# A gated-delta-rule block on one core: smaller pieces of two products, and a new order of the work on four engines

## The chip, the cores and the metric

The kernel runs on one NeuronCore of one Trainium2 chip. The metric is the device time of one launch in microseconds (us). Three timed runs of the kernel before gave 1795.96, 1807.67 and 1810.20 us; their median, 1807.67 us, is the time to beat. Lower is better. Everything is computed in 32-bit floats.

## The reference

The input is `hidden`, 2 sequences of 4096 tokens with 256 channels. Three residual parts follow each other, each on a layer norm of what came before:

```python
def ffn(x, W_r, W_k, W_v, mu_r, mu_k):
    x_prev = shift x by one token
    xr = mu_r * x + (1.0 - mu_r) * x_prev
    xk = mu_k * x + (1.0 - mu_k) * x_prev
    return sigmoid(xr @ W_r.T) * (square(relu(xk @ W_k.T)) @ W_v.T)

def attn(x):
    q, k, v = (silu(causal_conv4(x @ W.T)) for W in (Wq, Wk, Wv))   # 16 heads of 16
    q, k = l2norm(q) * 16 ** -0.5, l2norm(k)
    beta, g = sigmoid(x @ Wb.T), -exp(A_log) * softplus(x @ Wa.T + dt_bias)
    # per head, token after token, S is 16 x 16:
    #   S = S * exp(g_t);  S = S + k_t (outer) beta_t * (v_t - k_t . S);  o_t = q_t . S
    return (rmsnorm(o) * norm_w * silu(x @ Wg.T)) @ Wo.T

x = x + 0.5 * ffn(layernorm(x)); x = x + attn(layernorm(x)); x = x + 0.5 * ffn(layernorm(x))
```

The recurrence over S is computed in chunks of 16 tokens: inside a chunk a small triangular system is solved, and from chunk to chunk one 16 x 16 state per head and sequence is handed on.

## The kernel before

The 4096 tokens are cut into 32 groups of 128 tokens (`GROUPS`), both sequences together; a group has 32 packs (`PACKS`), each 16 tokens of 8 heads of one sequence, and 8 chunks (`NCH`). Each engine runs its own written-out list of segments in a loop over `step`. A segment such as `on(wo, step - 4)` works on group `step - 4`, so at any time some five groups are in flight, each at another stage. There is no scheduler at run time: the order is the order of the lines, and engines meet through semaphores that count up (`wait_ge`). Below, "step" is one turn of TensorE's loop.

The stages of a group g on TensorE (PE), by their function names: `turn1`, `ffn1_k`, `ffn1_r`, `ffn1_v` (first feed-forward part); `turn2`, `k_proj`, `q_proj`, `v_proj`, `gate` (projections); `k_squares`, `decay_sums`, `decay_steps`; `gram0` to `gram3` (products of keys and queries inside a chunk); `t_product` (the inverse of the triangular system, solved on VectorE, times the masked products); `d_product0` to `d_product3` (the write product: for each pack the part of the state transition and of the output that the solved system gives); `b_product` (what the values of each chunk write to the state); `chain` 0 to 7 (the hand-over of the state, chunk after chunk); `o_product` 0 to 7 (outputs); `o_squares`, `wo`; `turn3`, `ffn3_r`, `ffn3_k`, `ffn3_v`.

All small products go through the helper `pairs` (line 241), which splits the 128 x 128 array into square tiles as wide as the stationary operand: 64 x 64 tiles for `gram`, `d_product` and `o_product`, 32 x 32 tiles for `t_product`, `b_product` and `chain`. Everything else uses the full array. A 32-bit matmul is two passes, so a trace counts two records for each matmul.

Each result in PSUM lies in one of 8 banks, named by the table `PS`, and is read by one segment of another engine. The segments that the prediction speaks of:

- VectorE (DVE): `d_out0` to `d_out3` (lines 1180, 1201, 1219, 1231; they write `MQ` from `GQ` and the four write products), `chain` n (line 1105; copies the state behind chain step n from PSUM to `SA`, where the next chain step reads it), `conv_k`, `conv_q`, `conv_v` (line 1073, six instructions each), `gram0` to `gram3` (three instructions each, into `GK` and `KD`), `a_turn` (1387), `solve_mul` and `solve_sub` 0 to 14 (1090, 1095), `t_turn` (1111), `x1`, `x2`, `x3` (residual sums, 1395, 1237, 1138), `stats1` to `stats3`, `mix_k3`, `mix_r3` (1301, 1060), `o_norm` (1145).
- ScalarE (ACT): `t_out0`, `t_out1` (into `WP`), `tap_k`, `tap_q`, `tap_v`, `gate`, `o_square`, `norm1` to `norm3`, `yt`, and `silu_set` and `ln_exp_set`, which load one of two function tables (lines 627, 624).
- GpSimd (POOL): `o_sum`, `gate_norm`, `square3` and elementwise masks.

In the kernel before, `chain` n waits for the state copy of step n - 1 (`ch_s`) and, for n = 0, for all four `d_out` (`mt`); `b_product` came in four parts of two chunks, all of them ahead of the chain, and only its first part waited for `ch_s`.

## Time and profile before

| | |
|---|---|
| median of 3 runs | 1807.67 us (1795.96 to 1810.20) |
| the profiled execution, its own time | 1813.92 us |
| its span, first to last instruction | 1812.1 us |
| busy share PE / DVE / ACT / POOL | 95% / 72% / 58% / 26% |
| mean granted TensorE clock | 0.967 of 2.4 GHz |
| loop turns of PE | 37 |

The profiled execution was 6.3 us longer than the median of the timed runs. Its span and its time differ by 1.8 us. PE is busy nearly throughout, and the rest of its time is spread over many short gaps, so what an edit is worth is read from the starts of PE's blocks in order of time, not from the busy share.

### The profile page before, as it was taken

How to read it: one execution, taken by the hardware profiler on the slowest of the kernel's cores; microseconds unless marked ns; L12 is line 12 of the kernel's file. 1: busy time of each engine (PE TensorE's matmuls, PEld its weight loads, DVE VectorE, ACT ScalarE, POOL GpSimd, SP SyncE). 2: the span in 40 equal slices, each digit the busy share in tenths (PEclk: the TensorE clock that was granted, in tenths of full speed). 3: DMA queues.
4: the chain of work that ended last, by engine and by line, in shares of the span. 5: the costliest groups of instructions: out<-in, count | busy, mean ns of one | idle time of the engine just before them, and what ended most of it. 6: DMA issues, size and time to landing. Idle time of an engine off the chain costs nothing.

```text
span 1812.1 us, 100548 instructions
## 1 busy us (share of the span) xinstructions
PE 1715.9 (95%) x45056; PEld 1457.9 (80%) x45056; DVE 1299.3 (72%) x3718; ACT 1054.2 (58%) x2157; POOL 474.5 (26%) x389
## 2 busy tenths in 40 slices
PE   5799999999999999999999999999999999999986
PEld 3588888888888888888888888888888888888775
DVE  3777777787777777777778777777877777877531
ACT  4556656665666655566566566565656556655432
POOL 0223332222333221333222133322123323212201
PEclk9899999999999999999999999999999999999766
DMA  3000000000000000000000000000000000000000
GB/s 117 1 4 4 16 15 4 15 15 15 16 15 15 4 15 15 16 15 16 4 16 15 15 16 15 15 4 15 15 15 15 16 4 9 10 9 10 10 9 12
DMA packets 21582, 26.42 MB, mean 15 GB/s; under 512 B 2209, under 2 KB 20769, under 8 KB 21153
## 3 DMA queue, kind: packets, MB, share of 16 engines
q1 hardware_dynamic: 21152, 19.99, 3.4%
q8 instruction: 356, 5.83, 1.3%
q14 instruction: 74, 0.60, 0.1%
HBM read 11.60 MB, written 8.39 MB: 11 GB/s over the span
## 4 chain that ended last, share of the span: by engine, by line
PE 83%; issue 9%; DVE 5%; ACT 1%; POOL 1%; DVEq 0%; POOLq 0%; ACTq 0%
PE ps L241 38%; PE ps L223 16%; PE ps L232 10%; PE ps L216 6%; PE ps L454 3%; PE ps L209 2%; PE ps L404 2%; PE ps L552 2%; PE ps L352 2%; PE ps L544 2%; PE ps L370 1%; DVE XK L1060 1%; DVE XR L1301 1%; DVE SA L1105 1%; DVE KD L1343 1%
## 5 line engine op out<-in xcount | busy, mean ns | idle before, releaser
L241 PE MATMUL ps<-MQ,S 64*64 64x16 f32 x4096 | 255.3, 211 | 0.6 <-ACT S L621 0.6
L241 PE MATMUL ps<-WP,V 64*64 64x16 f32 x4096 | 252.9, 210 | 0.0
L241 PEld LDWEIGHTS ps<-MQ,S 64*64 64x64 f32 x4096 | 213.5, 140 | 45.7 <-issue 44.0
L1073 DVE SCALAR_TENSOR_TENSOR CV<-ps,cw,CV 128x256 f32<-128x256 f32 x576 | 233.8, 476 | 7.0 <-ACT CV L670 7.0
L241 PEld LDWEIGHTS ps<-WP,V 64*64 64x64 f32 x4096 | 214.4, 141 | 0.0
L999 POOL COPY TZ<-t_one 128x512 f32<-128x512 f32 x32 | 19.5, 609 | 727.0 <-DVE T L1111 727.0
L241 PEld LDWEIGHTS ps<-SA,MQ 32*32 32x32 f32 x8192 | 92.2, 109 | 72.1 <-issue 37.6
L241 PE MATMUL ps<-KQI,K 64*64 64x48 f32 x4096 | 138.7, 222 | 4.1 <-issue 3.8
L241 PE MATMUL ps<-SA,MQ 32*32 32x16 f32 x8192 | 117.3, 182 | 26.0 <-DVE SA L1105 20.7
L223 PE MATMUL ps<-w_r_ffn,XR 128*128 128x256 f32 x512 | 133.8, 406 | 2.3 <-DVE XR L1060 2.3
L216 PE MATMUL ps<-XK,w_k_ffn 128*128 128x256 f32 x512 | 128.5, 396 | 7.8 <-DVE XK L1060 7.8
L241 PEld LDWEIGHTS ps<-KQI,K 64*64 64x64 f32 x4096 | 129.6, 137 | 7.4 <-issue 5.5
L241 PE MATMUL ps<-WP,KD 64*64 64x48 f32 x4096 | 134.3, 220 | 1.3 <-issue 1.1
L1090 DVE TENSOR_TENSOR prod<-A,TZ 128x30 f32<-128x30 f32 (+7 forms) x480 | 121.3, 253 | 15.5
L241 PEld LDWEIGHTS ps<-WP,KD 64*64 64x64 f32 x4096 | 125.7, 135 | 8.1 <-issue 7.0
L1095 DVE TENSOR_TENSOR TZ<-TZ,prod 128x30 f32<-128x30 f32 (+7 forms) x480 | 121.2, 253 | 10.3
L223 PE MATMUL ps<-w_v_ffn,XK 128*128 128x256 f32 x512 | 126.2, 390 | 1.2 <-DVE X L1237 0.9
L241 PEld LDWEIGHTS ps<-GK,T 32*32 32x32 f32 x8192 | 86.1, 107 | 48.1 <-issue 35.4
L749 ACT ACTIVATE XR<-ps 128x512 f32<-128x512 f32 x32 | 19.1, 597 | 177.2 <-PE ps L223 177.2
L1145 DVE SCALAR_TENSOR_TENSOR OT<-ps,headp,GS 128x512 f32<-128x512 f32 x32 | 24.0, 751 | 129.2 <-POOL GS L969 129.2
L216 PEld LDWEIGHTS ps<-XK,w_k_ffn 128*128 128x128 f32 x512 | 98.8, 199 | 22.1 <-DVE XK L1060 5.9
L241 PE MATMUL ps<-GK,T 32*32 32x32 f32 x8192 | 102.8, 196 | 13.7 <-issue 7.8
(138 smaller groups left out, 3835.7 us busy)
## 6 DMA issues: line engine op xcount, KB each, us to landing
X<-in_x SPq DMA_DIRECT2D x32, 256.0 KB, 2.9
out_x<-X SPq DMA_DIRECT2D x32, 256.0 KB, 2.3
KQI<-in_blocks SPq DMA_DIRECT2D x2, 256.0 KB, 4.2
w_r_ffn<-in_wT_r_ffn SPq DMA_DIRECT2D x1, 256.0 KB, 3.3
w_k_ffn<-in_wT_k_ffn SPq DMA_DIRECT2D x1, 256.0 KB, 3.6
w_v_ffn<-in_wT_v_ffn SPq DMA_DIRECT2D x1, 256.0 KB, 4.5
w_k<-in_wT_k SPq DMA_DIRECT2D x1, 256.0 KB, 4.5
w_q<-in_wT_q SPq DMA_DIRECT2D x1, 256.0 KB, 4.7
```

The source lines that it names most:

```text
L209: last = nc.tensor.transpose(ps[:, dst * BANK + (k * B + b) * P:dst * BANK + (k * B + b + 1) * P], src[:, b * H + k * P:b * H + (k + 1) * ...
L216: last = mm(ps[:, dst * BANK + m * HB:dst * BANK + (m + 1) * HB], wt[:, k, m * P:(m + 1) * P], src[:, k * HB:(k + 1) * HB], start=(k == 0) ...
L223: last = mm(ps[:, dst * BANK + b * H:dst * BANK + (b + 1) * H], src[:, k * HB + b * TG:k * HB + (b + 1) * TG], wt[:, k, :], start=(k == 0) ...
L232: last = mm(ps[:, o:o + B * (CT + TG)], wt[:, k, m * P:(m + 1) * P], YT[:, k].rearrange("p b t -> p (b t)"), start=(k == 0), stop=(k == M ...
L241: last = mm(ps[rows, o:o + n], stat[rows, pk].rearrange("p s c -> p (s c)"), mov[rows], **flags)
L352: last = mm(ps[:, o:o + P], ST[:, c0:c0 + P], cum_i, start=True, stop=True)
L404: last = mm(ps[:, o:o + P], GB[:, c0:c0 + P], cum_i, start=True, stop=True)
L454: last = mm(ps[:, o:o + HB], w["g"][:, k, m * P:(m + 1) * P], YT[:, k, :, CT:], start=(k == 0), stop=(k == M - 1))
L544: mm(bank(PS["ssk"]), same_head, SK[:], start=True, stop=True).then_inc(s["ssk_ps"], 1)
L1073: stt(d4[:, m], src, cw[:, i, m, tap:tap + 1], d4[:, m], ALU.mult, ALU.add).then_inc(signal, 1)
L1090: tt(pr, a_j, t_j, ALU.mult).then_inc(s["sol"], 1)
L1095: tt(t_i, t_i, pr, ALU.subtract).then_inc(s["sol"], 1)
```

## The change

No arithmetic is changed and no matmul is added or taken away (22,720 on either side). What is changed:

1. `t_product` is issued in eight parts of four packs in place of four parts of eight, with other segments between them.
2. `b_product(g, n)` is one chunk, eight parts in all; part n waits for the state copy of chain step n - 1 and stands right ahead of `chain` n, or with one projection between them.
3. `d_product0` and `d_product1` move from the end of the step before to the start of the step in which `d_product2` and `d_product3` run: all four stand in a row, and `b_product` 0 and `chain` 0 right behind them. `d_product3` shares a bank with `d_product1` and waits for `d_out1`.
4. PSUM banks are dealt anew (`PS`), and with them the waits that guard a bank's reuse. `ffn3_r` now waits for `x1` of the newest group.
5. The lists of all four engines are in a new order. `ffn3_v` runs one step earlier, so that PE has 36 turns. ACT has four function table loads in a turn in place of two.
6. `o_product` is on 64 x 64 tiles, eight parts, before and after alike; only its neighbours change.

```diff
-            def b_product(g, q):
-                if q == 0:
+            def b_product(g, n):
+                if n == 0:
                     pe.wait_ge(s["wp"], 2 * g + 2)
                     pe.wait_ge(s["vt"], g + 1)
-                if g and q == 0:
-                    pe.wait_ge(s["ch_s"], 8 * g)
+                if g or n:
+                    pe.wait_ge(s["ch_s"], NCH * g + n)
                 w2 = WP[g % 2][:, :, 0:U].rearrange("p k (s c) -> p k s c", s=2)
-                for n in range(2 * q, 2 * q + 2):
-                    for ub in range(M * B):
...
             def t_product(g, q):
                 if q == 0:
                     pe.wait_ge(s["tp"], g + 1)
-                pe.wait_ge(s["gram_used"], 4 * g + q + 1)
+                pe.wait_ge(s["gram_used"], 4 * g + q // 2 + 1)
...
-                for pk in range(q * RING, (q + 1) * RING):
+                for pk in range(q * RING // 2, (q + 1) * RING // 2):
...
             def d_product3(g):
                 pe.wait_ge(s["wp"], 2 * g + 2)
                 pe.wait_ge(s["gram_used"], 4 * g + 4)
-                if g < GROUPS - 1:
-                    pe.wait_ge(s["cv"], 6 * g + 12)
-                    pe.wait_ge(s["tapv"], g + 2)
-                if g >= GROUPS - 1:
-                    pe.wait_ge(s["xt3"], g - 1)
+                pe.wait_ge(s["mt"], 4 * g + 2)
...
             def ffn3_r(g):
                 pe.wait_ge(s["xr3"], g + 1)
-                if g < GROUPS - 2:
-                    pe.wait_ge(s["e"], g + 3)
-                if g >= GROUPS - 1:
-                    pe.wait_ge(s["th3"], g)
+                if g < GROUPS - 4:
+                    pe.wait_ge(s["x1"], g + 5)
+                if g >= GROUPS - 4:
+                    pe.wait_ge(s["x2"], g + 1)
...
-            for step in range(GROUPS + 5):
-                on(wo, step - 4)
-                on(k_proj, step - 1)
-                on(b_product, step - 3, 0)
+            for step in range(GROUPS + 4):
+                on(d_product0, step - 3)
+                on(d_product1, step - 3)
                 on(d_product2, step - 3)
                 on(d_product3, step - 3)
+                on(b_product, step - 3, 0)
+                on(chain, step - 3, 0)
...
```

How the order moves, first on PE around the write product (`WP,KD`), the values' part (`VT,WP`) and chain step 0 (`SA,MQ`). Before, from `o_squares` on:

```order
L552 MATMUL ps<-OSQ,cst 128x512
L241 MATMUL ps<-GK,T 32x32 x32
L209 MATMUL ps<-cst,XN 128x128 x4
L241 MATMUL ps<-WP,KD 64x48 x32
L241 MATMUL ps<-GK,T 32x32 x32
L223 MATMUL ps<-w_o,OT 128x256 x4
L232 MATMUL ps<-YT,w_k 128x262 x4
L241 MATMUL ps<-VT,WP 32x16 x32
L241 MATMUL ps<-WP,KD 64x48 x32
```

Now, from `o_squares` on:

```order
L544 MATMUL ps<-OSQ,cst 128x512
L241 MATMUL ps<-GK,T 32x32 x16
L209 MATMUL ps<-cst,XN 128x128 x4
L241 MATMUL ps<-WP,KD 64x48 x64
L241 MATMUL ps<-VT,WP 32x16 x16
L241 MATMUL ps<-SA,MQ 32x16 x16
L347 MATMUL ps<-cst,ST 128x128 x4
L209 MATMUL ps<-cst,XN 128x128 x4
L232 MATMUL ps<-YT,w_k 128x262 x4
L223 MATMUL ps<-w_o,OT 128x256 x4
```

The write product's 64 matmuls are now in one run, and chain step 0 follows them with only 16 matmuls between.

The same place on DVE, now, from `x3` on (`MQ` rows are `d_out0` to `d_out3`, the first `SA` row is the copy of the last chain step of the group before, the second that of step 0):

```order
L1140 SCALAR_TENSOR_TENSOR XR<-XR,ps 128x512 [waits x2,xn3,v3_ps,th3]
L1141 SCALAR_TENSOR_TENSOR X<-XR,X 128x512 [waits vec_step]
L1182 TENSOR_TENSOR MQ<-GQ,ps 128x384 [waits o_ps,qp,ch_ps,gi,kd_ps]
L1203 TENSOR_TENSOR MQ<-GQ,ps 128x384 [waits qp,o_ps,gi,ch_ps,kd_ps,mt]
L1209 SCALAR_TENSOR_TENSOR nmr<-mv,rstd 128x2 [waits xn1,rstd1]
L1147 SCALAR_TENSOR_TENSOR OT<-ps,headp,GS 128x512 [waits wo_ps,rg]
L1221 TENSOR_TENSOR MQ<-GQ,ps 128x384 [waits qp,o_ps,gi,ch_ps,kd_ps,mt]
L1107 COPY SA<-ps 128x4x16 [waits s_slots,ch_ps]
L1233 TENSOR_TENSOR MQ<-GQ,ps 128x384 [waits qp,o_ps,gi,ch_ps,kd_ps,mt]
L1107 COPY SA<-ps 128x4x16 [waits s_slots,ch_ps]
```

The copy of the last chain step has moved from the middle of a solve to between `d_out2` and `d_out3`, and `o_norm` stands ahead of `d_out2`. The copy of step 3, before, stands behind `mix_k3`:

```order
L1301 TENSOR_TENSOR XR<-XT 128x512 [waits x3,r3_ps,v3_ps,xt3]
L1060 SCALAR_TENSOR_TENSOR XK<-XR,mu,XT 128x256 [waits vec_step]
L1060 SCALAR_TENSOR_TENSOR XK<-XR,mu,XT 128x256
L1105 COPY SA<-ps 128x4x16 [waits ch_ps]
L1358 TENSOR_TENSOR GK<-ps,E 128x8x32 [waits kd_ps,eg,t_ps,em,a4,gram_ps,gram_used]
```

Now it is the copy of step 6 that stands behind `mix_k3`, and `mix_r3` and `x1` follow it:

```order
L1303 TENSOR_TENSOR XR<-XT 128x512 [waits x3,r3_ps,v3_ps,xt3]
L1062 SCALAR_TENSOR_TENSOR XK<-XR,mu,XT 128x256 [waits vec_step]
L1062 SCALAR_TENSOR_TENSOR XK<-XR,mu,XT 128x256
L1097 TENSOR_TENSOR TZ<-TZ,prod 128x2x13x3 [waits sol]
L1172 SCALAR_TENSOR_TENSOR cz<-Z,cz 128x64 [waits sp]
L1107 COPY SA<-ps 128x4x16 [waits ch_ps]
L1092 TENSOR_TENSOR prod<-A,TZ 128x96 [waits sol]
L1062 SCALAR_TENSOR_TENSOR XR<-XR,mu,XT 128x256 [waits x3,r3_ps,xk3]
L1062 SCALAR_TENSOR_TENSOR XR<-XR,mu,XT 128x256
L1097 TENSOR_TENSOR TZ<-TZ,prod 128x2x12x4 [waits sol]
L1092 TENSOR_TENSOR prod<-A,TZ 128x110 [waits sol]
L1397 SCALAR_TENSOR_TENSOR XR<-XR,ps 128x512 [waits stats1,xn1,v1_ps,th1]
```

The sum `x1` of the newest group, for which `ffn3_r` on PE now waits, closes this run.

## Rows read from the trace of the kernel before

**Rows 1.** The page: busy time, instructions, and the granted clock in 40 slices.

```profile
PE 1715.9 (95%) x45056; PEld 1457.9 (80%) x45056; DVE 1299.3 (72%) x3718; ACT 1054.2 (58%) x2157; POOL 474.5 (26%) x389
...
PEclk9899999999999999999999999999999999999766
```

**Rows 2.** PE in order of time: start, us, block; `k_proj` 27 steps apart.

```profile
199.20 1.93 PE L232 MATMUL ps<-YT,w_k 128*128 128x262 f32 x8
...
1639.85 1.93 PE L232 MATMUL ps<-YT,w_k 128*128 128x262 f32 x8
```

**Rows 3.** PE's waits: us in total, times, longest.

```profile
PE ps L241 <- issue: 22.2, 41, 1.6
PE ps L241 <- DVE SA L1105: 20.7, 54, 2.0
```

**Rows 4.** PE in order of time, blocks of one step and the next.

```profile
902.34 1.99 PE L223 MATMUL ps<-w_v_ffn,XK 128*128 128x256 f32 x8
904.26 0.73 PE L241 MATMUL ps<-VT,WP 32*32 32x16 f32 x64
904.85 0.44 PE L241 MATMUL ps<-SA,MQ 32*32 32x16 f32 x32
...
929.71 1.89 PE L223 MATMUL ps<-w_v_ffn,XK 128*128 128x256 f32 x8
...
948.07 0.72 PE L241 MATMUL ps<-VT,WP 32*32 32x16 f32 x64
948.72 2.07 PE L241 MATMUL ps<-WP,KD 64*64 64x48 f32 x64
950.72 0.66 PE L209 MATMUL ps<-cst,XN 128*128 128x128 f32 x4
```

**Rows 5.** PE in order of time, chain steps 4 and 6 in another step.

```profile
1178.95 2.07 PE L241 MATMUL ps<-KQI,K 64*64 64x48 f32 x64
1181.37 0.44 PE L241 MATMUL ps<-SA,MQ 32*32 32x16 f32 x32 [0.35 <-DVE SA L1105]
...
1184.46 0.44 PE L241 MATMUL ps<-SA,MQ 32*32 32x16 f32 x32 [0.36 <-DVE SA L1105]
```

**Rows 6.** DVE in order of time, the same steps as rows 4.

```profile
912.37 0.68 DVE L1301 TENSOR_TENSOR XR<-XT 128x512 f32<-128x512 f32 x1
...
913.88 0.22 DVE L1105 COPY SA<-ps 128x64 f32<-128x64 f32 x1
...
915.14 0.22 DVE L1105 COPY SA<-ps 128x64 f32<-128x64 f32 x1
...
919.02 1.06 DVE L1387 STREAM_TRANSPOSE A<-GK 128x512 f32<-128x512 f32 x1
...
946.40 0.69 DVE L1237 TENSOR_TENSOR X<-X,ps 128x512 f32<-128x512 f32 x1 [1.65 <-PE ps L223]
947.13 0.75 DVE L1039 BATCH_NORM_STATS2 st<-X 128x6 f32<-128x256 f32 x2
...
950.89 0.55 DVE L1231 TENSOR_TENSOR MQ<-GQ,ps 128x384 f32<-128x384 f32 x1 [0.38 <-PE ps L241]
951.36 2.44 DVE L1073 SCALAR_TENSOR_TENSOR CV<-ps,cw,CV 128x256 f32<-128x256 f32 x6
```

**Rows 7.** Groups of instructions: busy us, mean ns of one | idle before.

```profile
L1090 DVE TENSOR_TENSOR prod<-A,TZ 128x30 f32<-128x30 f32 (+7 forms) x480 | 121.3, 253 | 15.5
...
L1395 DVE SCALAR_TENSOR_TENSOR XR<-XR,ps 128x512 f32<-128x512 f32 x32 | 22.0, 688 | 32.9 <-PE ps L223 29.8 <-issue 3.2
```

**Rows 8.** ACT in order of time, a change of function table near the start.

```profile
19.82 1.28 ACT L627 ACT_TABLE_LOAD   x1
21.12 0.60 ACT L749 ACTIVATE XR<-ps 128x512 f32<-128x512 f32 x1
```

**Rows 9.** PE in order of time, the last step.

```profile
1800.65 3.68 PE L216 MATMUL ps<-XK,w_k_ffn 128*128 128x256 f32 x8 [2.37 <-DVE XK L1060]
1804.16 1.89 PE L223 MATMUL ps<-w_r_ffn,XR 128*128 128x256 f32 x8
```

More of the change, by code:

```diff
@@ L569, in _ @@
-                on(decay_steps, step - 2)
-                on(ffn1_k, step)
-                on(chain, step - 3, 1)
-                on(gram0, step - 2)
+                on(chain, step - 3, 3)
                 on(gram1, step - 2)
-                on(chain, step - 3, 2)
-                on(turn3, step - 4)
-                on(chain, step - 3, 3)
                 on(gram2, step - 2)
                 on(gram3, step - 2)
+                on(b_product, step - 3, 4)
+                on(v_proj, step - 1)
@@ L1013, in _ @@
             for step in range(GROUPS + 4):
+                on(o_sum, step - 4)
+                on(stat1, step - 2)
+                on(g_diag, step - 2)
+                on(gate_norm, step - 4)
+                on(e_mask, step - 2)
                 on(g_ident, step - 2)
@@ L1463, in _ @@
+                on(chain, step - 3, 1)
+                on(conv_k, step - 1)
+                on(stats3, step - 4)
+                on(mix_r1, step)
+                on(chain, step - 3, 2)
+                on(gates_in, step - 1)
+                on(conv_q, step - 1)
+                on(chain, step - 3, 3)
+                on(gram0, step - 2)
+                on(gram1, step - 2)
+                on(soft_low, step - 1)
+                on(shift3, step - 4)
                 on(gram2, step - 2)
+                on(soft_part, step - 1)
```

374 lines of the change are left out of this document (185 added, 189 removed).

## The prediction

> **What bounds the kernel now.** I read the page first, for the busy shares and the granted clock [rows 1]: PE is busy 95% of the span, no other engine over 72%, and the granted clock is at 0.9 to 1.0 of 2.4 GHz except in the last tenth. So the kernel is bound by TensorE's stream of instructions. The busy share says little about edits, so I then read PE's blocks in order of time and measured from start to start. `k_proj` starts at 199.20 and, 27 steps later, at 1639.85 [rows 2]: 53.36 us a step. Thirty-two groups at that pace are nearly the whole time.
>
> Adding up the start-to-start times of all blocks of one step, each at its usual, undisturbed value, gives 51.5 us. The other 1.86 us are gaps. The list of waits names two releasers [rows 3]. One is the state copy on DVE. Chain step 4 waits for it regularly: gram blocks of 64 records take 2.00 (948.72 to 950.72 shows the same for the write product [rows 4]) but 1178.95 to 1181.37 is 2.42, with the copy named [rows 5], because that copy stands behind `mix_k3` on DVE. Chain step 6, right behind step 5, waits again for its copy: 0.36 shown, 0.43 measured from start to start [rows 5]. Together 0.85 a step. The rest, about 1.0, is mostly "issue", where PE waited for nothing that the trace shows, scattered over the blocks of small matmuls.
>
> **The change, part by part.** Sums are made against the profiled execution, 1813.9, and moved to the median at the end.
>
> *Fewer changes of tile size on PE.* A step has 36 runs of equal tile size before and 32 after, and the same 22,720 matmuls in all. What a change costs shows in two places. The same `v_ffn` block is busy 1.99 behind 32-wide tiles and 1.89 behind full-width work [rows 4]. `b_product` blocks take 0.59 when the 32-wide chain follows (904.26 to 904.85) and 0.65 when another size does (948.07 to 948.72) [rows 4]. So 0.06 to 0.10 for each, and four fewer save 0.3 a step. Cutting `t_product` into eighths and `b_product` into chunks costs no more than this count says; in themselves they are the same passes with a few more semaphore events.
>
> The Trainium skill (TensorEngine Tiling (Array Packing), Key Properties) says that changing the tiling mode drains TensorE. Taken as a whole matmul's latency, some 0.2 us by the mean of one small matmul, four fewer would save 0.8 us a step; the two pairs of rows above speak for a third of that.
>
> *The wait behind `mix_k3` goes.* The copy of step 3 now follows `conv_q` directly, and three gram blocks and a projection lie between chain steps 3 and 4. That takes 0.42 a step off. What is late next is treated below, since `mix_k3` has only been moved.
>
> *Chain step 4 to step 5.* In the new order `b_product` 5 stands right behind chain 4 and waits for its copy, with nothing between. It is the wait of steps 5 and 6 before: 0.43. Gone there, new here, zero net.
>
> *Write product to chain step 0.* This is the wait that the change adds. Before, `d_product3` was followed by some 7 us of other blocks ahead of chain 0. Now only `b_product` 0 (0.3) is between, and chain 0 needs `d_out3`. From the trace: the next block starts at 950.72, `d_out3` starts at 950.89 and is busy 0.55 [rows 4, 6], so chain 0 can start 0.72 + 0.05 after the product's block and `b_product` 0 covers 0.3: at least 0.47 of stall. More comes from the queue on DVE: `o_norm` (an instruction like those of L1395, 0.69 [rows 7]) stands ahead of `d_out2`, and the copy of the group's predecessor (0.22) between `d_out2` and `d_out3`; `b_product` 0 waits for that copy too. Counting from the start of the four products: `d_out1` ends at 2.7, `o_norm` at 3.5, `d_out2` at 4.1, the copy at 4.3, `d_out3` at 4.9, chain 0 at 5.0 in place of 4.3. So 0.7, between 0.47 and 0.95, the upper end if `gate_norm` on POOL hands over late. Behind the waiting chain 0 stand `decay_steps`, `turn1`, `k_proj` and all else of PE. I take 0.7, as the queue on DVE is plain from the order.
>
> *DVE between `x2` and `x1`.* In the new order PE's `ffn3_r` waits for `x1`, and DVE has a dense list from `x2` (which needs `wo`) to `x1`: `x2` 0.7, `stats3` 0.9, two convolutions of 2.4, `mix_r1` and `mix_r3` 0.8 each, `mix_k3` 1.5 (912.37 to 913.88), four gram segments of 1.15 (913.88 to 915.14 with a copy), `a_turn` 1.1, `x1` 1.35 [rows 6, 7], nine solve steps of 0.25 [rows 7], six copies of 0.2, and about 1.0 of tiny ones. Sum 21.0, and 0.3 for the hand-overs at both ends: 21.3. PE's work in the same stretch: five full-width blocks of 1.87, gram 4.0, seven pairs of `b_product` and chain at 0.67, and three short blocks (transposes, gate inputs, squares) 2.55, in all 20.6, plus the 0.43 above: 21.1. The two are equal within my error. PE's own scattered gaps in that stretch (some 0.4) partly hide behind DVE. I put down 0.15 for the wait at `ffn3_r`, between 0 and 0.6.
>
> *Two more function table loads.* A load is 1.28 and the next instruction starts 0.02 later [rows 8], so ACT gains 2.6 us of work a step on an idle share of 42%. What hides it: ACT has to do `relu3`, `rstd1`, `tap_v`, `norm2`, one load and `gate` between the end of `ffn3_k` and `ffn3_v`, which waits for `gate`'s bank. That is 4.8 us against 5.5 us of PE blocks there. It costs nothing while that cover of 0.7 holds. The other load lies ahead of `exp_q` and `t_out0`, which has some 2 us to spare.
>
> The Trainium skill (ScalarE: Activation LUTs, What ACT_TABLE_LOAD costs) gives about 1283 ns for the load and a drain of about 1380 ns on top. The trace agrees on the first; the second does not show in the rows above. With it the cover would be gone.
>
> *Everything else moved* has one answer: I went through the semaphores of each PE block against the last writer by the durations of the trace. The closest are `gram0` behind `conv_k` and `turn3` behind `gram3` on DVE (0.6 to 0.8 to spare) and `t_product` behind `t_turn` (1.2). POOL's queue (`t_start`, `square3`, `stat0`, `beta_diag`, `q_decayed`, `o_sum`) has `o_sum` ready about 1 us ahead of `o_squares`.
>
> Sum of a step: -0.3 - 0.42 + 0.7 + 0.15 = +0.13, times 32 = +4.
>
> *Both ends.* At the start PE waits for latencies, and ACT's two loads of 1.28 stand between `norm2` and `yt` of the second group: +3. At the end, `ffn3_r` stands ahead of `ffn3_k` on PE, while DVE makes `xk` first. In the last step `ffn3_k` ran 3.5 us at the low clock, with `ffn3_r` after it [rows 9] and the squaring of `xk` hidden behind that. Now both that relu and that square lie open, and `mix_r3` comes first: about +3. PE has one turn less, but the last group's path (`wo`, `x2`, `turn3`, `ffn3`) is the same, so nothing is gained there; `ffn3_v` of the group before the last now stands ahead of the last `o_squares`, mostly in the shadow of `o_sum`: +1.
>
> Total +4 + 3 + 4 = +11: 1825 for an execution like the profiled one, **1819** on the median (1807.67 + 11).
>
> **The rivals.**
>
> *DVE is late in the dense stretch (slower).* If DVE's list from `x2` to `x1` takes 0.5 us more than I sum, all of it lands at `ffn3_r`, or at the state copies before it, on every step: 32 x 0.5 = 16, so 1835. It decides from a list of 21.5 us on. For it: six state copies each wait for PE in order, and each late chain step delays DVE as well. Against it: PE's own gaps have to be overtaken first.
>
> *The gaps shrink (faster).* If `o_norm` is done early enough, the wait at chain 0 is 0.47 or less, and if a third of the 1.0 us of unexplained gaps falls into waits that exist anyway, the step is -0.3 - 0.42 + 0.45 - 0.3 = -0.57, 32 times is -18, with +7 at the ends: 1796. For it: pieces are now mixed with long blocks, and gaps sat in small ones. Against it: no row says what these gaps are.
>
> *Table loads are not hidden (slower).* If a load costs 1.4 us more than its row, `gate` comes 0.7 us after `ffn3_v` wants its bank: 32 x 0.7 = 22, so 1841. The row of a load followed at once by work speaks against it. This is the result by the skill's page on ScalarE named above.
>
> *The change does not do what it says.* "Output product on 64x64 tiles" is no change: the trace of before has it in 64*64 tiles already. I count nothing for it.
>
> **How the numbers follow.** Forecast 0.52 (its own range 1806 to 1830), DVE late 0.24, gaps shrink 0.19, table loads 0.05. From the slower rivals upwards the range is cut at 1842; from the faster one downwards at 1793; the range 1793 to 1842 leaves out some 2 in 10. A measurement of this kernel tells about 1% from no change, 1789.6 to 1825.7. Faster by over 1% takes a part of the faster rival: 0.11. Slower by over 1% takes nearly all of the two slower ones and a tenth of the forecast: 0.32. Within 1%: 0.57.
>
> **What the profile after would show.** The idle time before a `b_product` or chain block with a state copy as releaser, twice a step: 0.5 to 0.9 us at chain 0 (or `b_product` 0) behind the 128 records of the write product, and 0.4 at `b_product` 5. At `ffn3_r` of line 223, a wait for DVE's line 1397 or 1398 of 0 to 0.6. No wait of gram's successor on the copy. Step length, from `k_proj` to `k_proj`, 53.2 to 53.8. ACT's busy time up by some 95 us, with no wait of PE on ACT's `GS`. PE's busy time nearly the same, down by up to 10. I am wrong if steps are under 53 (then the copies or the gaps were dearer than I think) or over 54.2 (then DVE sets the pace), or if a wait stands where I found 1 us to spare.

## The result, and the profile after

The changed kernel takes **1856.39 us** (median of 4 runs, 1840.83 to 1868.65), the kernel before in the same measurement 1808.93 us. The ratio is **1.024 (1.019 to 1.029)**: slower by 2.4%. The forecast was 1819. An unchanged copy of the changed kernel on another chip took 1838.18, with 1796.08 for the kernel before, and a ratio of 1.022 (1.015 to 1.028). The profiled execution that follows is the slowest of its four and counts as a slow one; the execution in the third row of the table below does not.

The page of the kernel after (busy time and granted clock) answers to [rows 1]:

```profile
span 1866.6 us, 100566 instructions
PE 1756.2 (94%) x45056; PEld 1488.5 (80%) x45056; DVE 1352.3 (72%) x3718; ACT 1153.0 (62%) x2234; POOL 474.3 (25%) x389
PEclk8988999989999999998999999899999999899776
```

PE is busy 40 us longer with the same 45,056 records, and no wait adds to busy time. DVE is busy 53 us longer, also with the same instructions, and ACT 99 us longer: its 77 more instructions are function table loads of 1.28. The row of the granted clock has dips to 0.8 in the middle of the run, where [rows 1] has 9 throughout.

PE in order of time, the `k_proj` of the groups 0, 3 and 31 (answers to [rows 2]):

```profile
37.74 2.83 PE L232 MATMUL ps<-YT,w_k 128*128 128x262 f32 x6
...
161.96 1.94 PE L232 MATMUL ps<-YT,w_k 128*128 128x262 f32 x8
...
1699.87 1.94 PE L232 MATMUL ps<-YT,w_k 128*128 128x262 f32 x8
```

These three marks cut an execution into a start, 28 steady steps, and an end. The same marks in three profiled executions, with the mean granted clock of each:

| kernel | group 0 | group 3 | group 31 | span | one step | after group 31 | clock |
|---|---|---|---|---|---|---|---|
| before | 29.5 | 147.4 | 1639.8 | 1812.1 | 53.30 | 172.3 | 0.967 |
| after | 37.7 | 162.0 | 1699.9 | 1866.6 | 54.93 | 166.7 | 0.935 |
| after, another chip | 38.3 | 162.7 | 1666.0 | 1829.8 | 53.69 | 163.7 | 0.960 |

So of the 54.5 us between the first two rows, 14.6 come from the start, 45.4 from the steady steps, and the end gives 5.5 back. The third row is the same program as the second: the same order and the same waits, but 1.24 us a step apart. What differs is the clock. Span times (1 - clock) times 2 is the time spent at 1.2 GHz: 243 us against 146. For 97 us more of that, the span is 36.8 us longer, 0.38 us for each. The four runs of the kernel after fall in the order of their clocks too: 0.935, 0.943, 0.947 and 0.954 gave 1868.65, 1860.27, 1852.52 and 1840.83.

**Where the clock falls.** Stretches of one step of the kernel after (start and end, length, busy time of PE, PEld, DVE, ACT and POOL, then granted clock), and below them PE in order of time:

```profile
463.00:465.00 2.00, 2.00 (x14) 1.50 (x12) 1.28 (x5) 1.93 (x6) 0.00 (x0) 1.00 0.00 0
465.00:466.40 1.40, 1.40 (x50) 1.40 (x52) 1.36 (x8) 0.32 (x1) 0.00 (x0) 1.00 0.06 12
466.40:467.90 1.50, 1.50 (x53) 1.47 (x49) 1.33 (x8) 0.00 (x0) 0.00 (x0) 0.95 0.00 0
467.90:469.70 1.80, 1.80 (x5) 1.45 (x5) 1.80 (x2) 0.00 (x0) 0.00 (x0) 0.50 0.00 0
469.70:471.40 1.70, 1.70 (x7) 1.03 (x5) 0.64 (x2) 0.00 (x0) 0.61 (x1) 0.57 0.00 0
471.40:473.40 2.00, 2.00 (x69) 1.97 (x71) 0.13 (x1) 1.87 (x6) 1.23 (x2) 1.00 0.04 8
```

```profile
463.00 2.00 PE L442 MATMUL ps<-YT,w_g 128*128 128x256 f32 x8
...
467.84 3.62 PE L216 MATMUL ps<-XK,w_k_ffn 128*128 128x256 f32 x8
```

Behind `gate` stand three parts of `o_product` in a row (464.92 to 467.84), PE busy throughout and at 1.00. Towards their end the clock drops to 0.50, which is 1.2 GHz of 2.4, and stays there in most of the next two stretches; I call this a spell. The next block is `ffn3_k`, full-width: it takes 3.62 in place of 1.9. In this execution each step from group 6 to group 30 has such a spell, and each of the 25 begins in the last 0.2 us of the three parts or in the first 0.9 us of `ffn3_k`. Before, no more than two parts of `o_product` stood together: three pairs had a full-width block behind them, the last a quarter of `t_product`.

The group of the two feed-forward `_k` projections (busy us, mean ns | idle before) in the kernel before, after, and after on the other chip:

```profile
L216 PE MATMUL ps<-XK,w_k_ffn 128*128 128x256 f32 x512 | 128.5, 396 | 7.8 <-DVE XK L1060 7.8
```

```profile
L216 PE MATMUL ps<-XK,w_k_ffn 128*128 128x256 f32 x512 | 172.5, 496 | 2.5 <-DVE XK L1062 2.5
```

```profile
L216 PE MATMUL ps<-XK,w_k_ffn 128*128 128x256 f32 x512 | 147.5, 438 | 2.5 <-DVE XK L1062 2.5
```

From start to start `ffn3_k` takes 3.30 on average (median 3.50, 26 steps), and 2.36 on the other chip; undisturbed it is 1.92. The blocks behind it (`o_product`, `t_product`, `decay_sums`, `ffn3_v`) give 0.8 more a step, where the spell comes later or a second time. The mean of these 26 steps, 55.0, less 1.4 and 0.8 is 52.8. A second way gives nearly the same: the granted clock of the steady part is 0.959, so 126 us of it are at 1.2 GHz, and 44 on the other chip; 34.6 us in 28 steps for 82 is 0.42, and 54.93 - 0.42 x 126 / 28 is 53.0. So without the clock, the new order is by this estimate 0.3 to 0.5 us a step *shorter* than the old. The Trainium skill (TensorE: Matmul & The Clock Gate, Terms) counts half of the time at half clock as lost; these two executions show 0.38 to 0.42 of it.

**The write product and chain step 0.** PE, then DVE in order of time (answers to [rows 4] and [rows 6]):

```profile
481.78 4.01 PE L241 MATMUL ps<-WP,KD 64*64 64x48 f32 x128
485.98 0.44 PE L241 MATMUL ps<-VT,WP 32*32 32x16 f32 x32 [0.19 <-DVE SA L1107]
486.49 0.44 PE L241 MATMUL ps<-SA,MQ 32*32 32x16 f32 x32
486.86 1.16 PE L347 MATMUL ps<-cst,ST 128*128 128x128 f32 x8
```

```profile
483.95 0.56 DVE L1203 TENSOR_TENSOR MQ<-GQ,ps 128x384 f32<-128x384 f32 x1 [0.44 <-PE ps L241]
...
484.49 0.75 DVE L1147 SCALAR_TENSOR_TENSOR OT<-ps,headp,GS 128x512 f32<-128x512 f32 x1
485.15 0.55 DVE L1221 TENSOR_TENSOR MQ<-GQ,ps 128x384 f32<-128x384 f32 x1
485.61 0.22 DVE L1107 COPY SA<-ps 128x64 f32<-128x64 f32 x1
485.88 0.55 DVE L1233 TENSOR_TENSOR MQ<-GQ,ps 128x384 f32<-128x384 f32 x1
```

The queue on DVE is the one that I wrote down, and chain 0 starts 4.71 after the write product where the prediction had 4.3 without a wait: 0.4, not 0.7. `d_out3` ends at 4.65 and not 4.9, because DVE starts an instruction some 0.1 before the one ahead of it ends (485.15 to 485.61 is 0.46 for a busy time of 0.55).

**PE's waits** (us in total, times, longest; answers to [rows 3]):

```profile
PE ps L241 <- DVE SA L1107: 21.5, 63, 1.7
...
PE ps L241 <- DVE CV L1075: 14.1, 29, 3.4
...
PE ps L241 <- issue: 3.6, 10, 0.6
```

The waits for the state copy are as large as before, in other places. The gaps that nothing explained are down from 22.2 to 3.6 (8.5 on the other chip). And there is a wait that I had not forecast: `gram0` for `conv_k` on DVE. From start to start, chain 2 ahead of `gram0` takes 0.79 in place of 0.38 in nearly every step. The wait for `x1` shows in the same way: chain 7 to `ffn3_r` takes 0.60, of which 0.22 is wait.

**Why `conv_k` is late.** DVE in order of time, then POOL, in another step of the kernel after:

```profile
707.64 1.38 DVE L1254 TENSOR_TENSOR XR<-XT 128x512 f32<-128x512 f32 x1 [1.01 <-ACT XT L647]
709.05 2.46 DVE L1062 SCALAR_TENSOR_TENSOR XK<-XR,mu,XT 128x256 f32<-128x256 f32 x2
...
712.17 2.42 DVE L1075 SCALAR_TENSOR_TENSOR CV<-ps,cw,CV 128x256 f32<-128x256 f32 x6
```

```profile
707.20 1.27 POOL L1005 TENSOR_TENSOR E<-E,msk 128x512 f32<-128x512 f32 x1 [5.16 <-ACT E L689]
708.43 2.41 POOL L951 TENSOR_TENSOR GQ<-pair,EQ 128x1024 f32<-128x1024 f32 x1
```

The same two instructions in the kernel before, DVE:

```profile
901.58 0.69 DVE L1252 TENSOR_TENSOR XR<-XT 128x512 f32<-128x512 f32 x1
902.30 0.88 DVE L1060 SCALAR_TENSOR_TENSOR XK<-XR,mu,XT 128x256 f32<-128x256 f32 x2
```

There POOL began its two multiplications at 907.09, when `mix_k1` was long done. In the new order they lie beside each other, and `mix_k1` takes 3.84 in place of 1.57. POOL's larger one takes 2.41 in place of 1.96. `conv_k` ends at 714.59, and `gram0` on PE starts behind it:

```profile
714.85 1.14 PE L241 MATMUL ps<-KQI,K 64*64 64x48 f32 x32 [0.34 <-DVE CV L1075]
```

The Trainium skill (SBUF — State Buffer, Who interferes with whom) says that a DVE instruction with two inputs in SBUF contends with a GpSimd instruction that reads SBUF, and that the port pair which they share is an exclusive lock. From 707.64 to 711.51 the four take 3.87. One after another they would take 0.83 (the rest of POOL's first) + 0.69 + 1.96 + 0.88 = 4.36; free of each other, 2.79. The trace is nearer to taking turns and doesn't quite reach it; a run below shows a plainer case.

### The profile page after: what moved, and what is told of

Read it like the earlier page. It is cut to its first block, busy times and chain, and to the rows that moved or that the text cites. A ratio compares the mean times of both kernels' runs of the same rounds, so it can differ in the third digit from the quotient of the medians.

```text
span 1866.6 us, 100566 instructions
## 1 busy us (share of the span) xinstructions
PE 1756.2 (94%) x45056; PEld 1488.5 (80%) x45056; DVE 1352.3 (72%) x3718; ACT 1153.0 (62%) x2234; POOL 474.3 (25%) x389
## 4 chain that ended last, share of the span: by engine, by line
PE 73%; DVE 14%; issue 8%; ACT 3%; DMA 1%; SPq 0%; POOL 0%; DVEq 0%; ACTq 0%; POOLq 0%
PE ps L241 37%; PE ps L223 13%; PE ps L216 8%; PE ps L232 3%; DVE CV L1075 3%; PE ps L442 3%; DVE XR L1254 2%; PE ps L391 2%; PE ps L209 2%; PE ps L347 2%; PE ps L544 2%; DVE XK L1062 1%; DVE X L1398 1%; DVE XR L1397 1%; DMA X<-in_x 1%
## 5 line engine op out<-in xcount | busy, mean ns | idle before, releaser
L216 PE MATMUL ps<-XK,w_k_ffn 128*128 128x256 f32 x512 | 172.5, 496 | 2.5 <-DVE XK L1062 2.5
L241 PEld LDWEIGHTS ps<-VT,WP 32*32 32x32 f32 x8192 | 91.8, 109 | 87.0 <-issue 62.5
L216 PEld LDWEIGHTS ps<-XK,w_k_ffn 128*128 128x128 f32 x512 | 119.8, 245 | 25.5 <-issue 2.8
L1140 DVE SCALAR_TENSOR_TENSOR XR<-XR,ps 128x512 f32<-128x512 f32 x32 | 22.0, 688 | 161.7 <-issue 158.4
L241 PE MATMUL ps<-VT,WP 32*32 32x16 f32 x8192 | 116.4, 182 | 22.2 <-DVE SA L1107 21.5
L223 PE MATMUL ps<-w_r_ffn,XR 128*128 128x256 f32 x512 | 129.8, 399 | 7.9 <-DVE XR L1062 3.3
L223 PE MATMUL ps<-w_v_ffn,XK 128*128 128x256 f32 x512 | 133.8, 407 | 2.1 <-POOL XK L959 1.9
L794 ACT ACTIVATE XK<-ps 128x512 f32<-128x512 f32 x32 | 19.1, 597 | 185.0 <-PE ps L216 185.0
L241 PE MATMUL ps<-WP,KD 64*64 64x48 f32 x4096 | 129.4, 219 | 1.0 <-ACT WP L856 0.6
```

The costliest lines, as they stand in the source:

```text
L216: last = mm(ps[:, dst * BANK + m * HB:dst * BANK + (m + 1) * HB], wt[:, k, m * P:(m + 1) * P], src[:, k * HB:(k + 1) * HB], start=(k == 0) ...
L223: last = mm(ps[:, dst * BANK + b * H:dst * BANK + (b + 1) * H], src[:, k * HB + b * TG:k * HB + (b + 1) * TG], wt[:, k, :], start=(k == 0) ...
L241: last = mm(ps[rows, o:o + n], stat[rows, pk].rearrange("p s c -> p (s c)"), mov[rows], **flags)
```

## The experiments

Each time is a median beside the kernel before on the same chip. First came three edits of the kernel after and one of the kernel before, all in the same measurement (before: 1794.30).

**Is the run of three what lowers the clock?** Part 4 goes behind `ffn3_k`.

```diff
                 on(o_product, step - 3, 3)
-                on(o_product, step - 3, 4)
                 on(ffn3_k, step - 4)
+                on(o_product, step - 3, 4)
                 on(o_product, step - 3, 5)
```

Ahead of `gate`, between it and `ffn3_k`, and behind that stand 2, 2 and 3 parts, in place of 2, 3 and 2.

> The changed kernel with one part of the output product moved: `ffn3_k` stands behind part 3 in place of part 4, so that the runs of `o_product` parts are 2, 2 and 3 long in place of 2, 3 and 2. Theory A (clock): in the profile after, the granted clock falls to 1.2 GHz once a step, at the end of the run of three parts, and `ffn3_k` takes 3.5 us in place of 1.9, with what follows also slower; together about 2.2 us a step. If the run of three right behind `gate` and the chain is what lets it fall, `ffn3_k` is back at 1.9, and unless the new run of three (now followed by two parts of `t_product`) does the same, the step is near 53 us and the time 1800 to 1810; if it does the same, the slow stretch moves to `decay_sums` and the time stays at 1840 to 1860. Theory B (waits): the time is lost in PE's waits for DVE (0.4 us at `gram0`, 0.2 at `ffn3_r`, 0.25 at `b_product` 0); these stay, and so does the time, within 5 us of 1856.

Measured: 1860.07, ratio 1.036 (1.031 to 1.042), clock 0.943. `ffn3_k` is back to 1.92, and the next full-width blocks behind the run of three have the spell now. The groups of `decay_sums` (L391), of the `_v` and of the `_k` projections:

```profile
L391 PE MATMUL ps<-cst,GB 128*128 128x128 f32 x256 | 51.2, 362 | 0.0
```

```profile
L223 PE MATMUL ps<-w_v_ffn,XK 128*128 128x256 f32 x512 | 145.2, 432 | 2.0 <-POOL XK L959 1.8 <-POOL XK L955 0.2
L216 PE MATMUL ps<-XK,w_k_ffn 128*128 128x256 f32 x512 | 135.4, 410 | 2.5 <-DVE XK L1062 2.5
```

After had 42.5, 133.8 and 172.5 there. All 14 spells of its 28 steady steps begin in the last 0.2 us of the run of three or within 1.2 us behind it. The spell follows the run; it doesn't belong to `ffn3_k`.

**Four pairs, as before.** `decay_sums` and part 7 ahead of the first parts of `t_product`, so that no more than two parts stand together.

```diff
-                on(o_product, step - 3, 4)
                 on(ffn3_k, step - 4)
+                on(o_product, step - 3, 4)
                 on(o_product, step - 3, 5)
+                on(decay_sums, step - 1)
                 on(o_product, step - 3, 6)
+                on(o_product, step - 3, 7)
                 on(t_product, step - 2, 0)
                 on(t_product, step - 2, 1)
-                on(decay_sums, step - 1)
-                on(o_product, step - 3, 7)
```

> The changed kernel with the output product in four pairs of parts: `ffn3_r`, parts 0 and 1, `gate`, parts 2 and 3, `ffn3_k`, parts 4 and 5, `decay_sums`, parts 6 and 7, then `t_product` 0 to 3 in a row. Theory A (clock): no stretch of a step at 1.2 GHz, mean granted clock back to 0.965 or more, a step of 52.9 us, 1790 to 1800 us. Theory B (waits for DVE): 1850 to 1860, clock as it comes.

Measured: 1854.54, ratio 1.033 (1.029 to 1.036), clock 0.957. The time at 1.2 GHz over the span is 160 us in place of 211 in the run above, yet the total hardly moves: `t_product` now comes as one long run of small tiles, PE has 27.0 us of "issue" gaps in the small matmuls in place of 5.2, and `ffn3_v`, right behind them, is at 143.5. Seven of the 12 spells in its steady steps begin inside this new run of small tiles (parts 6 and 7 and four of `t_product`). Two things changed at once here, so this run misses its forecast of 1790 to 1800 and says that pairs are not enough if the small blocks are then gathered elsewhere, and no more.

**Or is it the idle time at `ffn3_r`?** A rival: PE stands idle for `x1` at 459.1 in the step shown above, 8.6 us before the drop. `ffn3_r` goes behind the first part of `o_product`.

```diff
-                on(ffn3_r, step - 4)
                 on(o_product, step - 3, 0)
+                on(ffn3_r, step - 4)
                 on(o_product, step - 3, 1)
```

> The changed kernel with `ffn3_r` behind part 0 of the output product in place of ahead of it, so that the wait for `x1` (0.22 us of idle PE ahead of `ffn3_r`) is covered by part 0; the run of three parts ahead of `ffn3_k` stays. Theory A (the run of small-tile parts lets the clock fall): `ffn3_k` still takes about 3.5 us and the time is 1840 to 1855. Rival A2 (it is idle PE a little earlier that lets the clock fall): `ffn3_k` is back at 1.9 and the time at 1800 or less. Theory B (waits): 7 us less than the changed kernel, 1849.

Measured: 1875.29, ratio 1.041 (1.034 to 1.047), clock 0.933. Chain 7 to the next block is 0.43 in place of 0.60, so the wait is gone, and `ffn3_k` is slow as ever (mean 2.95 from start to start). So this wait is not the cause. The waits ahead of chain 0 and `gram0` are taken away in a run further down, and the spell stays there too.

**The same run in the kernel before.** Only `o_product` 4 is moved, ahead of `ffn1_r`, so that parts 2, 3 and 4 stand in a row.

```diff
                 on(o_product, step - 3, 3)
+                on(o_product, step - 3, 4)
                 on(ffn1_r, step)
                 on(ffn1_v, step)
-                on(o_product, step - 3, 4)
```

> The kernel before with one part of the output product moved ahead, so that parts 2, 3 and 4 stand in a run and `ffn1_r`, `ffn1_v` follow. Theory A (clock): a run of three parts alone is enough; `ffn1_r` behind it takes 3.5 us in place of 1.8, once a step, and the time goes up by 40 to 60 us to 1850 to 1870. If a run of three alone is not enough (the changed kernel has chain steps, a wait and only `gate` ahead of it), the time stays at 1805 to 1812. Theory B expects 1808 too.

Measured: 1819.72, ratio 1.012 (1.006 to 1.018), clock 0.960: 25 us lost by the place of 32 matmuls, where I had expected 40 to 60. `ffn1_r` takes 2.62 on average from start to start (median 2.95) in place of 1.83. Stretches, and PE in order of time:

```profile
401.80:403.70 1.90, 1.90 (x70) 1.90 (x66) 1.73 (x8) 0.00 (x0) 0.00 (x0) 0.99 0.05 9
403.73:405.50 1.77, 1.77 (x7) 1.50 (x5) 1.69 (x10) 0.00 (x0) 0.00 (x0) 0.50 0.00 0
405.50:407.30 1.80, 1.80 (x6) 1.42 (x6) 0.19 (x1) 0.00 (x0) 0.00 (x0) 0.56 0.00 0
407.30:409.30 2.00, 2.00 (x19) 1.51 (x18) 0.12 (x1) 1.91 (x5) 0.00 (x0) 1.00 0.00 0
```

```profile
403.73 3.63 PE L223 MATMUL ps<-w_r_ffn,XR 128*128 128x256 f32 x8
```

PE is busy 1.90 of 1.90 ahead of the drop. This is the picture of the kernel after, made in the kernel before with one line moved.

**The changed kernel again, the start, the halves, the waits.** Four kernels in one measurement on another chip (before: 1796.08). The first is the kernel after without an edit.

> The changed kernel itself, unaltered, on the chip of the next three, so that they can be read against it. Both theories expect the ratio measured before, 1.019 to 1.029 of the kernel before, with a spell of about 3.4 us at 1.2 GHz in most steps.

Measured: 1838.18 (1827.56 to 1868.51), ratio 1.022 (1.015 to 1.028), its marks in the table above. The same program spreads over 41 us here.

*Table loads only in the steps that use them:*

```diff
-                ln_exp_set()
+                if 2 <= step < GROUPS + 5:
+                    ln_exp_set()
```

and the same with `3 <= step < GROUPS + 3` around the two loads between `norm2` and `yt`, and `1 <= step < GROUPS + 5` at the last one.

> The changed kernel without the function table loads that nothing uses: none in ScalarE's first turn, one in its second, two in its third, and none of the middle pair at the end of the program. PE's first instruction started at 16.80 us in place of 12.02 and the first `k_proj` at 37.74 in place of 29.50. Theory: the loads of 1.28 us that stand ahead of the first `norm1` (some four more than before) and two ahead of the first `yt` are that loss; the first PE instruction then starts at 11 to 12 us, the first `k_proj` at about 30, and the time is 7 to 9 us under the changed kernel. Rival: the start came late because of the input's transfers; then PE starts at 16 to 17 again and nothing is gained.

Measured: 1836.58, ratio 1.022 (1.016 to 1.028). The first block of PE starts at 9.74, not 17.36 as in the unchanged kernel of this measurement (16.80 in the page above):

```profile
9.74 1.08 PE L209 MATMUL ps<-cst,XN 128*128 128x128 f32 x4 [9.74 <-ACT XN L641]
```

The fourth `k_proj` starts at 151.8 in place of 162.7, so 10.9 us of the start are these loads. The total doesn't show it, for a step was 53.97 in this execution and 53.69 in that of the unchanged kernel. A gain of 10 us is smaller than what the clock does to this order from run to run.

*Halves:* `gate` and `ffn3_k` are each issued as two halves (of four matmuls), with one part of `o_product` between any two halves.

```diff
-                on(gate, step - 1)
+                on(gate, step - 1, 0)
                 on(o_product, step - 3, 2)
+                on(gate, step - 1, 1)
                 on(o_product, step - 3, 3)
+                on(ffn3_k, step - 4, 0)
                 on(o_product, step - 3, 4)
-                on(ffn3_k, step - 4)
+                on(ffn3_k, step - 4, 1)
```

> The changed kernel with `gate` and `ffn3_k` each issued in two halves (4 of 8 passes each), laid between single parts of the output product: parts 0, 1, half `gate`, part 2, half `gate`, part 3, half `ffn3_k`, part 4, half `ffn3_k`, parts 5 and 6. Same matmuls, four more changes of tile size (0.3 us a step, +10 us). Theory A (clock): the run of three parts is gone and full-width work lies between each; `ffn3_k`'s halves run at full clock, and the time at 1.2 GHz in the middle of the program falls from about 120 us to under 60, unless the stretch from part 5 through `t_product` becomes the place; time 15 to 30 us under the changed kernel. Theory B (waits): 10 us over it.

Measured: 1839.57 (1839.08 to 1845.52), ratio 1.024 (1.021 to 1.028), clock 0.964. The steady steps are at a clock of 1.00 and the spread is gone, but each half costs 1.06 where half a block took 0.96, and each lone part 1.04 where half a pair took 0.99. A step is 53.60, and this execution's end was 10 us longer than the unchanged kernel's, at a lower clock there (0.75 against 0.79). So the remedy works on the clock and costs what it gives: 0.42 x 44 / 28 is 0.7 us a step won, and four halves and three lone parts cost 0.6. I had expected 15 to 30 us less.

*Waits covered:* `decay_steps` and `turn1` go between the write product and `b_product` 0, and `ffn1_k` ahead of `gram0`.

```diff
-                on(b_product, step - 3, 0)
-                on(chain, step - 3, 0)
                 on(decay_steps, step - 2)
                 on(turn1, step)
+                on(b_product, step - 3, 0)
+                on(chain, step - 3, 0)
...
-                on(gram0, step - 2)
                 on(ffn1_k, step)
+                on(gram0, step - 2)
```

> The changed kernel with `decay_steps` and `turn1` moved between the write product and `b_product` 0, and `ffn1_k` moved ahead of `gram0`. Covered are the waits of PE at `b_product` 0 and chain 0 (some 0.3 to 0.45 us a step) and at `gram0` for `conv_k` (0.41). Theory B (the loss is waits): 0.8 us a step, 25 us, under the changed kernel. Theory A (clock): the blocks read back at 0.27 for `b_product` 0 and 0.38 for chain 2, but the spell at 1.2 GHz stays once a step in or around `ffn3_k`, and with it most of the loss; 10 to 25 us under the changed kernel, and still over the kernel before.

Measured: 1813.77 (1809.19 to 1814.63), ratio 1.009 (1.006 to 1.012), 24 us below the unchanged kernel. PE in order of time:

```profile
945.36 4.01 PE L241 MATMUL ps<-WP,KD 64*64 64x48 f32 x128
949.30 1.16 PE L347 MATMUL ps<-cst,ST 128*128 128x128 f32 x8
950.82 0.44 PE L241 MATMUL ps<-VT,WP 32*32 32x16 f32 x32
951.10 0.45 PE L241 MATMUL ps<-SA,MQ 32*32 32x16 f32 x32
```

Chain 2 to the next block is 0.38 again (0.79), `b_product` 0 to chain 0 is 0.28 (0.51), and the write product 3.94 (4.20). That is 0.9 a step; the steps show 0.60, 53.09 against 53.69. All 12 spells of its steady steps still begin at the run of three.

This run also moves DVE and POOL against each other, which its edit does not say. POOL, then DVE in order of time:

```profile
952.40 1.96 POOL L951 TENSOR_TENSOR GQ<-pair,EQ 128x1024 f32<-128x1024 f32 x1
```

```profile
952.48 2.02 DVE L1284 TENSOR_TENSOR eg<-eg,pair 128x128 f32<-128x128 f32 x1
954.43 0.68 DVE L1254 TENSOR_TENSOR XR<-XT 128x512 f32<-128x512 f32 x1
```

POOL's large multiplication now meets a small product of two SBUF operands on DVE, which starts 0.08 after it, ends 0.14 behind it, and takes 2.02 in place of 0.29 (mean 1857 ns in place of 292). POOL's takes its 1.96. Here DVE waits until POOL's whole instruction is over; in 29 of the 32 groups it ends 0.14 to 0.15 behind it. The two instructions of `mix_k1` lie behind and are back at 22.5 and 58.0 us with `mix_k3`'s (42.4 and 103.9 in the unchanged kernel). In this step `conv_k` ends at 959.11, just before 959.26, where `gram0` would have stood; so in this step that alone would have taken nearly all of the wait away, without `ffn1_k` ahead of it.

**Put together.** Three kernels in one measurement, twelve runs each (before: 1808.11 over 29 runs). The first joins the edit of the table loads and that of the covered waits.

```diff
+                if 2 <= step < GROUPS + 5:
+                    ln_exp_set()
...
+                on(decay_steps, step - 2)
+                on(turn1, step)
                 on(b_product, step - 3, 0)
                 on(chain, step - 3, 0)
-                on(decay_steps, step - 2)
-                on(turn1, step)
...
+                on(ffn1_k, step)
                 on(gram0, step - 2)
-                on(ffn1_k, step)
...
```

> The changed kernel with both edits together: function table loads only where they are used, and `decay_steps`, `turn1` and `ffn1_k` moved to cover PE's waits. If the two add up: 10 us less at the start, 0.65 us less a step (18 us), so some 28 us under the changed kernel, 1808 to 1812 where the kernel before is at 1796, with 50 to 120 us of the middle still at 1.2 GHz. Ratio about 1.005. If the first edit's 10 us at the start are given back elsewhere (its ratio did not move), 1.009 as without it.

Measured: 1810.99, ratio 1.001 (0.998 to 1.004), clock 0.954. Level with the kernel before, at a lower granted clock: 0.943 to 0.958 in its twelve runs, 0.961 to 0.981 in those of the kernel before beside it.

The next adds `ffn3_k` in two halves around part 4, so that the parts stand 2, 2, 1, 2, 1 with something full-width between.

```diff
                 on(o_product, step - 3, 3)
+                on(ffn3_k, step - 4, 0)
                 on(o_product, step - 3, 4)
-                on(ffn3_k, step - 4)
+                on(ffn3_k, step - 4, 1)
```

> The kernel of the run before it, with `ffn3_k` alone in two halves around part 4 of the output product, so that no three parts stand in a run. Costs 0.2 us a step in changes of tile size (6 us). Theory A (clock): the middle of the program has under 30 us at 1.2 GHz; every 10 us less there are 4 us less of time, so 10 to 20 us gained and 6 paid: 1798 to 1804, ratio 0.998 to 1.003. If the clock has nothing to do with it: 6 us slower than the run before it.

Measured: **1796.74** (1789.33 to 1802.91), ratio **0.993 (0.991 to 0.996)**, clock 0.967. By its ratio it is the fastest of all, 0.7% below the kernel before, and its interval leaves out 1. The group of the `_k` projections, and the stretches around part 4:

```profile
L216 PE MATMUL ps<-XK,w_k_ffn 128*128 128x256 f32 x512 | 142.1, 412 | 2.5 <-DVE XK L1068 2.5
```

```profile
919.59:920.60 1.01, 1.01 (x8) 0.68 (x4) 0.91 (x6) 0.00 (x0) 0.00 (x0) 1.00 0.00 0
920.60:921.70 1.10, 1.10 (x34) 1.02 (x33) 1.10 (x1) 0.00 (x0) 0.00 (x0) 1.00 0.00 0
921.70:922.80 1.10, 1.10 (x9) 0.72 (x6) 1.10 (x2) 0.00 (x0) 0.20 (x1) 1.00 0.00 0
```

Its steady steps are 52.64 each, 0.66 under the kernel before, at a clock of 1.00 like it. Against the kernel of the run before it, in the same measurement, that is 14 us and 0.87 a step for no spell in place of 75 us at 1.2 GHz, with 0.3 a step paid for the pieces.

The third adds the halves of `gate` too.

```diff
-                on(gate, step - 1)
+                on(gate, step - 1, 0)
                 on(o_product, step - 3, 2)
+                on(gate, step - 1, 1)
                 on(o_product, step - 3, 3)
```

> The same with `gate` in two halves as well, as in the earlier run with halves. Theory A (clock): under 15 us at 1.2 GHz in the middle, and another 0.25 us a step paid: 1800 to 1808, and the narrowest spread of its times among the three, since what varies from run to run is the time at 1.2 GHz. If the clock is no cause: 12 us slower than the first of the three.

Measured: 1809.29 (1802.94 to 1814.53), ratio 1.001 (0.999 to 1.004), clock 0.968. The run behind `gate` was only two parts by now, so there was no clock to win. A step is 53.02, 0.38 more; the pieces account for 0.3 of it (`gate` 2 x 1.06 for 1.92, two lone parts of 1.04 for a pair of 1.97).

Last, the wait at `b_product` 5, with `turn3` as its cover, in the kernel with loads, waits and the halves of `ffn3_k` (before: 1801.25 over 17 runs).

```diff
                 on(chain, step - 3, 4)
+                on(turn3, step - 4)
                 on(b_product, step - 3, 5)
                 on(chain, step - 3, 5)
-                on(turn3, step - 4)
```

> The kernel with loads where used, waits covered and `ffn3_k` in halves, and `turn3` moved between chain 4 and `b_product` 5, where PE waits 0.42 us a step for the state copy. If PE sets the pace there, the step is 0.4 us shorter, 13 us in all, ratio 0.986. If DVE's dense list from `x2` to `x1` sets it (the rival of the prediction), the wait at `ffn3_r` (now 0.22 us) grows by what is saved, to about 0.6, and the time stays at a ratio of 0.992 to 0.994.

Measured: 1800.22, ratio 1.000 (0.998 to 1.002): no gain, and worse than either forecast; without this edit the ratio was 0.993, and the step 52.64 in place of 52.74. PE's waits in it:

```profile
PE ps L224 <- DVE X L1404: 9.0, 25, 0.7
PE ps L242 <- DVE SA L1113: 6.2, 11, 1.9
...
PE ps L209 <- DVE KD L1387: 5.7, 19, 0.8
```

The copy's wait has shrunk to 6.2 (16.8 in the kernel that it is made from), and `ffn3_r` waits 9.0 for `x1` and `turn3` itself 5.7 for `gram3`. Chain 7 to `ffn3_r` went from 0.60 to 0.76 (medians). In this stretch it is DVE's list that sets the pace, and a wait taken away on PE comes back at the list's end.

**The spells, counted.** In the 28 steady steps of each profiled execution; "at the run" means that the spell begins in the last 0.3 us of three parts in a row, or within 1.2 us behind them:

| kernel | spells | at the run | us at 1.2 GHz | one step |
|---|---|---|---|---|
| before | 1 | no run of three | 3 | 53.30 |
| before, part 4 moved | 16 | 15 | 55 | 54.04 |
| after | 25 | 25 | 126 | 54.93 |
| after, another chip | 10 | 9 | 44 | 53.69 |
| after, part 4 behind `ffn3_k` | 14 | 14 | 99 | 54.29 |
| after, `ffn3_r` behind part 0 | 22 | 21 | 116 | 54.77 |
| after, waits covered | 12 | 12 | 51 | 53.09 |
| loads and waits | 16 | 16 | 75 | 53.51 |
| loads, waits, halves of `ffn3_k` | 0 | no run of three | 0 | 52.64 |

A run of three does not bring a spell in every step, and no row says why one step has it and another has not.

## Why the prediction was wrong

**The step that failed** is the first one: "the granted clock is at 0.9 to 1.0 of 2.4 GHz except in the last tenth. So the kernel is bound by TensorE's stream of instructions." I took the clock as a property of the run and priced every block of PE at its row of before. But the order of blocks sets the clock. The change puts three parts of `o_product` in a row, and in most steps the clock falls to 1.2 GHz at the end of them. In the profiled execution this costs by estimate 1.9 to 2.2 us a step by the two counts above, 53 to 62 us in 28 steps. That is more than the 45.4 lost there, since the order in itself saves the rest. One line moved in the kernel before brings it about there, and splitting `ffn3_k` around a part takes it away; neither adds arithmetic. None of my rivals had it.

These figures are of the slowest execution. In the one on the other chip the spells cost less, 0.42 x 44 = 19 us in 28 steps by the same estimate, and the start, 15.3 us longer than before, nearly as much. So the start, priced at +3, is the second step that failed. The repairs say the same: splitting `ffn3_k` gave 14 us, the loads 10.9 at the start, and covering two waits 24, while the clock's repair by both halves alone gave nothing. What part each has in a median time is not shown more closely.

Without the clock, the sum of a step against what was found:

| term | forecast | found |
|---|---|---|
| four changes of tile size fewer | -0.3 | not measured apart, -0.3 kept |
| wait behind `mix_k3` gone | -0.42 | gone: `gram1` to `gram3` take 2.93 and `b_product` follows without a wait |
| chain 4 to `b_product` 5 in place of 5 to 6 | 0 | 0.80 against 0.38 at the new place; 0.42 come and 0.43 go, 0 net |
| write product to chain 0 | +0.7 | +0.45 (0.41 against the 4.3, 0.49 by the run with the waits covered) |
| `ffn3_r` for `x1` | +0.15 | +0.22 |
| `gram0` for `conv_k` | 0 ("0.6 to 0.8 to spare") | +0.41 |
| unexplained gaps | 0 | 22.2 to 3.6 in all, -0.6 a step (-0.4 on the other chip) |
| sum | +0.13 | -0.2 by these terms; 52.8 to 53.0 against 53.30 is -0.3 to -0.5 |

- *Chain 0* was mis-sized: I added up DVE's busy times, which overlap by 0.1 from one instruction to the next.
- *`gram0`* failed because I priced `mix_k1` by its row of before. Moved beside POOL's multiplications it takes 2.3 us more. Over the run, its two groups are busy 103.9 + 42.3 us where they were 56.4 + 21.9. That this is what makes `gram0` wait rests on the order of times above and on the run with the waits covered, where `mix_k1` is back at its row of before and `conv_k` ends in time; `ffn1_k` was moved in the same edit, so the two are not told apart.
- *The gaps shrink* was a rival with 0.19, and its mechanism came true: "issue" fell from 22.2 to 3.6, and the wait at chain 0 was about its 0.47. Its -0.57 a step came to -0.3 or so, for the wait at `gram0` is in none of its terms; the time went the other way by the clock and the start.
- *DVE late in the dense stretch* (0.24) came true in part: 0.22 at `ffn3_r` where I had 0.15, and the last experiment shows that DVE's list is at its limit there.
- *Table loads not hidden* did not come true in the steady steps: no wait of PE on ACT's `GS` beyond 1.3 us in all.
- *The start* was forecast at +3 and came to +14.6. I counted the two loads of one step. In the first steps, most segments have nothing to do, but the loads are outside of `on` and are issued all the same: eight loads stand ahead of the first `norm1` where four stood before, which makes PE start at 16.80 and not at 12.02, and two stand between `norm2` and the first `yt`. The experiment with the loads gave 10.9 back; its fourth `k_proj` is still at 151.8 where the kernel before has 147.4, and those 4.4 stay open.
- *The end* was forecast at +4 and came to -5.5. It swings with the clock by more than that: 159.4 after group 31 in the kernel before with one part moved, 172.3 in the kernel before itself, 181.1 in the kernel after with `ffn3_r` moved. So neither the forecast nor its miss can be read from it.
- ACT's busy time rose by 98.8, as forecast (95). PE's was to fall by up to 10 and rose by 40 at a clock of 0.935; on the other chip, at 0.960, it was 1713.8, or 2 less than before.

What stays open: why the clock falls in 25 of 28 steps in one execution and in 10 in another of the same program, and why in some steps a spell is longer. That the place of a part of `o_product` sets it is shown, in both directions; what in that run of blocks counts is not.

## What to carry to other kernels

When an edit regroups a TensorE stream, look at what stands side by side, not only at the sum: a full-width block behind a longer run of small matmuls may run at half the clock, although no engine ever waits. Compare PE's busy time for the same instructions before and after, and the granted clock in stretches of 2 us; if they differ, no account of waits will find the loss. A duration is only worth its row while the other engine's neighbour in time is the same, and DVE beside POOL is the pair to check.
